# A conv and mixture-of-experts kernel: the first stage written in another order on four engines

## The reference

```
x = x + conv(ln_c(x))        # ln_c: mean and variance over the 192 channels
t = tokens(x)
t = t + ffn(ln_t(t))         # ln_t: the same over a token's 192 numbers
```

```
h   = xg @ W1[e]                     # 192 -> 1024
act = h[..., :512] * silu(h[..., 512:])
ye  = act @ W2[e]                    # 512 -> 192, weighted, added to the token
```

## Time and profile before

| | |
|---|---|
| median of three runs | 230.23 us (229.35 to 232.94) |
| the profiled execution | 229.77 us |
| its span, first to last instruction | 228.0 us |
| PE busy | 205.2 us (90%) |
| DVE busy | 160.2 us (70%) |
| ACT busy | 128.3 us (56%) |
| POOL busy | 118.7 us (52%) |
| mean granted clock of PE | 0.952 |

### The profile page before, as it was taken

How to read it: one execution, slowest core, us unless ns; L and a number is a source line. 1 busy time by engine, 2 the same in 40 slices (tenths; PEclk the granted TensorE clock), 3 DMA queues, 4 the chain that set the end, 5 groups by cost and what they waited for, 6 DMA issues and landing times.

```text
span 228.0 us, 4487 instructions
## 1 busy us (share of the span) xinstructions
PE 205.2 (90%) x1351; PEld 188.3 (83%) x1351; DVE 160.2 (70%) x509; ACT 128.3 (56%) x320; POOL 118.7 (52%) x130
## 2 busy tenths in 40 slices
PE   7998799869858999999999999999999999999930
PEld 2786699653327999999999999999999999999920
DVE  2674989998704599598598678679778868956520
ACT  2454765374202476587578578577568658745510
POOL 5102212100077154885877787687687683185184
PEclk9999999976795899999999999999999999999995
DMA  6648375879724392494395386288278253034043
GB/s 206 183 123 236 69 204 164 188 195 294 169 73 105 69 289 66 68 286 98 43 262 132 56 252 135 52 175 212 55 139 236 69 52 31 0 36 49 0 46 42
DMA packets 28015, 29.40 MB, mean 129 GB/s; under 512 B 6915, under 2 KB 24544, under 8 KB 28000
## 3 DMA queue, kind: packets, MB, share of 16 engines
q1 hardware_dynamic: 18656, 17.28, 26.6%
q0 software_dynamic: 7680, 9.05, 23.7%
q10 hardware_dynamic: 1664, 2.88, 4.8%
HBM read 19.86 MB, written 9.35 MB: 128 GB/s over the span
## 4 chain that ended last, share of the span: by engine, by line
PE 71%; DVE 11%; DMA 7%; POOL 3%; ACT 3%; issue 2%; SPq 1%; POOLq 0%; DVEq 0%; ACTq 0%
PE low L1173 6%; PE bank L1173 5%; PE first L1157 4%; PE first L1154 4%; PE first L1150 4%; PE first L1158 4%; PE first L1151 4%; PE low L1157 4%; PE low L1158 4%; PE low L1154 4%; PE low L1151 4%; PE low L1150 4%; PE both L1173 3%; PE low L1175 2%; PE bank L1175 2%
## 5 line engine op out<-in xcount | busy, mean ns | idle before, releaser
L500 POOL DMA_INDIRECT out<-y,goal x40 | 65.9, 1648 | 36.6 <-DVE y L933 27.4
L480 POOL DMA_INDIRECT rows<-rows_dram,source x40 | 42.5, 1062 | 36.2 <-DMA rows_dram<-row 18.9
L902 DVE TENSOR_TENSOR al<-act,ah 128x308 fp32r<-128x308 f32 x64 | 30.1, 471 | 1.0
L635 ACT CAST ah<-act 128x308 fp32r<-128x308 f32 x64 | 28.3, 443 | 1.8 <-DVE act L910 1.8
L910 DVE TENSOR_TENSOR act<-low,sil 128x308 f32<-128x308 f32 x32 | 15.3, 479 | 12.8 <-ACT sil L642 12.8
L642 ACT ACTIVATE sil<-first 128x308 f32<-128x308 f32 x32 | 13.7, 428 | 16.7 <-PE first L1158 15.6
L642 ACT ACTIVATE sil<-low 128x308 f32<-128x308 f32 x32 | 13.7, 428 | 14.2 <-PE low L1158 13.3
L910 DVE TENSOR_TENSOR act<-first,sil 128x308 f32<-128x308 f32 x32 | 15.3, 479 | 8.0 <-ACT sil L642 7.2
L1150 PE MATMUL first<-xh_a,hi_a 128*128 128x308 f32 x64 | 20.1, 314 | 0.7 <-ACT xh_a L625 0.7
L1157 PE MATMUL first<-x_b,hi_b 128*128 128x308 f32 x64 | 20.1, 314 | 0.0
L1154 PE MATMUL first<-xl_a,hi_a 128*128 128x308 f32 x64 | 19.9, 312 | 0.1
(11 more groups left out here) (172 smaller groups left out, 562.3 us busy)
## 6 DMA issues: line engine op xcount, KB each, us to landing
raw_b<-w SPq DMA_DIRECT2D x12, 256.0 KB, 4.1
raw_a<-w SPq DMA_DIRECT2D x6, 512.0 KB, 5.3
raw<-w SPq DMA_DIRECT2D x6, 384.0 KB, 6.1
gram_dram<-gram SPq DMA_DIRECT2D x8, 230.0 KB, 3.2
xt<-x_tokens SPq DMA_DIRECT2D x4, 384.0 KB, 4.4
out<-xt SPq DMA_DIRECT2D x4, 384.0 KB, 5.1
rows_dram<-row SPq DMA_DIRECT2D x3, 386.0 KB, 4.3
raw_b<-w ACTq DMA_DIRECT2D x4, 256.0 KB, 4.2
```

The costliest lines, as they stand in the source:

```text
L480: G.indirect_dma_start(out=rows[b][:, t, :], out_offset=None, in_=rows_dram, in_offset=bass.IndirectOffsetOnAxis(ap=source[:, n:n + 1], ax ...
L500: nc.gpsimd.indirect_dma_start(out=out, out_offset=bass.IndirectOffsetOnAxis(ap=goal[0:m, n:n + 1], axis=0), in_=y[0:m, t, :], in_offset=N ...
L635: nc.scalar.copy(ah[:, j, lo:hi], act[n % 3][:, 0:hi - lo]).then_inc(a_hi, 1)
L902: V.tensor_tensor(al[:, j, lo:hi], act[n % 3][:, 0:hi - lo], ah[:, j, lo:hi].bitcast(F32), ALU.subtract).then_inc(a_lo, 1)
```

## The change

Only stage 1 changes; every computation stays, but for the seven fillers.

- ACT: both halves of `take_gram(1)` and `deviation(3)` come before `take_corr(0)`, and the load of W1 of expert 0 behind it. The loads of expert 1 and `take_corr(3)` come before `deviation_b(2)` and `normed(2)`.
- PE: the 7 fillers after `grams(1)` go. `turn_corr(1)` stands between the halves of `grams(2)`.
- DVE: in the last group, `residual` and `stats_b` come ahead of the choice. `choose` is split in `best_scores` and the rest, `row_scales` in `row_shifts` and `row_gaps`.
- SP: `store_rows(2)` comes before `store_x1(1)`.

```diff
@@ SP
             store_x1(0)
+            store_rows(2)
             store_x1(1)
-            store_rows(2)
@@ ACT
             deviation(2)
+            take_gram(1)
+            deviation(3)
+            take_corr(0)
             load_w1(s, 0, 0)
-            take_gram(1, (0,))
-            take_corr(0)
-            deviation(3)
-            take_gram(1, (1,))
             features(2)
...
                 split_hi(0, 0, n)
-            deviation_b(2)
-            take_corr(3)
-            normed(2)
             load_w1(s, 1, 1)
             load_w2(s, 1, 1)
+            take_corr(3)
+            deviation_b(2)
+            normed(2)
@@ DVE
+            def best_scores(g):
                 for t in range(TILES):
                     last = V.max(top[:, t, :], score[:, t, :])
                 then(last)
+            def choose(g):
                 for t in range(TILES):
                     last = V.max_index(top_e[:, t, :], top[:, t, :], score[:, t, :])
...
                 combine(g)
-                choose(g)
-                residual(g)
-                stats_b(g)
                 if g + 1 < GROUPS:
+                    best_scores(g)
+                    choose(g)
+                    residual(g)
+                    stats_b(g)
                     find_slots(g)
-                    row_scales(g)
+                    row_shifts(g)
+                    row_gaps(g)
                 else:
-                    row_scales(g)
+                    residual(g)
+                    stats_b(g)
+                    best_scores(g)
+                    row_shifts(g)
+                    choose(g)
+                    row_gaps(g)
                     find_slots(g)
                 spots(g)
@@ PE
-            def grams(g):
+            def grams(g, halves=(0, 1)):
...
-                for t in range(TILES):
+                for t in [2 * h + i for h in halves for i in range(2)]:
...
             grams(1)
-            keep_busy(BUSY_FIRST, bank[0])
             turn_corr(0)
             conv_rest(0)
             turn_f(2)
             places(0)
-            grams(2)
+            grams(2, (0,))
             turn_corr(1)
+            grams(2, (1,))
```

More of the change, by code:

```diff
@@ L770, in stats_b @@
                 last.then_inc(var_b, 1)
-            def choose(g):
+            def best_scores(g):
                 for t in range(TILES):
@@ L806, in find_slots, with row_shifts @@
                 then(V.tensor_scalar(lane[:, :], slot[:, :], P - 1, None, ALU.bitwise_and))
-            def row_scales(g):
+            def row_shifts(g):
                 v.wait_ge(sqrt_b, g + 1)
@@ L813, in row_scales, with row_gaps @@
                                        in1=rstd_b[:, tiles(g)], op0=ALU.mult, op1=ALU.mult).then_inc(shift_ready, 1)
+            def row_gaps(g):
                 then(V.tensor_tensor(unit[:, :], norm[:, tiles(g)], rstd_b[:, tiles(g)], ALU.mult))
@@ L957, in _ @@
             T = nc.tensor
-            BUSY_START, BUSY_FIRST, BUSY_LAST, BUSY_TABLE, BUSY_END = 20, 7, 6, 14, 24
+            BUSY_START, BUSY_LAST, BUSY_TABLE, BUSY_END = 20, 6, 14, 24
             def keep_busy(n, idle):
```

## The result

The changed kernel takes **237.03 us** (median of 5, 234.59 to 237.31) against 230.23 (229.16 to 232.94): the ratio is 1.030 with a 95% interval of 1.025 to 1.035. I had forecast 231.2 and a range up to 233.6.

A forecast was written before the change was run, and what follows sets the result against it. It took the start of POOL's first gather to decide, released by the last row stores, with DVE's order from `conv_rest(1)` behind them. Sum: 229.77 - 0.4 + 1.9 - 0.1 = 231.2 us, range 228.2 to 233.6.

The forecast's parts named there:

- The rest: ACT's early loads of expert 1, `take_corr(3)` ahead of `deviation_b(2)`, SP's `store_rows(2)` first, fillers behind the table: summed as nothing.
- Part 1 and 2: Stage 1 up to `conv_rest(1)`: group 1's gram copied sooner, -0.4 us; PE's clock falling without the 7 fillers, +1.9 us.
- Part 1: Gram of group 1: second half copied 2.75 us sooner, so `conv_rest(1)` ends 0.4 us sooner, at 31.6.
- Part 3: Last group: row stores land at 60.6, but slow fillers delay row numbers to 61.65, which release the gather: -0.1 us.
- `near` of group 1 was late: Rival: W1 transfers delay `near` to 27.0, `conv_rest(1)` ends 0.5 us later at 32.6; 230.2 with clock held, chance 0.1.
- The slower case: Rival: PE's clock falls and stays low until group 2's convolution, PE becomes the bound: +5, 234.3 us, chance 0.12.

The follow-up runs named there:

- the last part alone: Kernel before with only the last group's `residual` and `stats_b` ahead of its choice, and `store_rows(2)` ahead of `store_x1(1)`: 232.97 us, ratio 1.011.

## Why the prediction was wrong

**The step that failed** is in "The rest": ACT's early loads of expert 1 were costed at nothing, "and a few tenths if `near(3)` is slowed, also under DVE's queue". The cover I named, DVE's queue, was only some 2.5 us deep: from `near(3)` at 42.9, the correlations (0.9), transposes (0.65), copy (0.6) and convolution (1.7) lead to 46.8, and DVE comes to group 3's scores at 49.3. It was used up by a transfer that I took to be slowed by tenths: `near(3)` was there at 50.7, 7.8 us later. Some 1.4 of these stood already when the gram went out, 3.8 came in its second store and 2.5 in the load of `near`. Then PE, idle for 5.28 us, made the transposes and the convolution at half clock, 2.1 us more than the 3.9 above. 7.8 - 2.5 + 2.1 is 7.4, and group 3's scores came 7.46 late. That last term, too, stands nowhere in my sum. I had the very row for the first, 4.9 against 2.6 us for a gram beside W1, and applied it to group 1 only. The loss is shown by undoing the loads (3.8 and 4.0 us back in the time), by doing them alone (from group 2's scores to group 3's 13.49 us in place of 8.60) and by issuing them on SP just behind `near(3)` (8.60 again). That the rows of group 0 add to it is shown by the landing of the gram's stores, 5.5 and 5.1 us with them ahead, 2.4 and 2.7 without. And behind `take_corr(3)`, `deviation_b(2)` was named as harmless; the run with the old order shows that it was.

**Part 1 and 2** were forecast together at +1.5, and `conv_rest(1)` ended 1.43 us late, at 33.50, with the clock at 0.50 for 6.8 us from 22.2 on. That the sum fits is luck, for both terms missed and the errors cancel. The run with the loads put back has the same front at full clock and ends `conv_rest(1)` at 32.32: so Part 1 is worth +0.25 and not -0.4, and the low stretch +1.2 and not +1.9. The cause I gave, the lost fillers, is not borne out as a cost: with them back the low stretch was half as long, and nothing came back. The gap of 1.65 us that the issues of W1 on ACT open before the features of group 2 is new too, but it is argued and not shown as the cause, since that same run has it and kept its clock.

Nor does the clock fall in the changed kernel alone. Of the six traces with its front and no fillers, five have a low stretch, of 6.8 us each, and one has none. Of the seven with the old front, four have none, the kernel before among them, and three have one of 3.4 us: the last part alone (0.50 between 27.3 and 30.7), the loads on SP (25.8 to 29.3) and the loads moved alone (26.5 to 29.9), whose rows read:

```profile
26.00:27.00 1.00, 0.63 (x2) 0.63 (x3) 0.96 (x4) 1.00 (x3) 0.00 (x0) 0.74 0.46 102
...
29.00:30.00 1.00, 1.00 (x6) 1.00 (x5) 0.68 (x5) 0.65 (x2) 0.44 (x2) 0.56 0.00 0
```

One profile is not enough to say whether a stretch keeps its clock, and two traces of different kernels can differ here by 2 us for no reason of their code.

**Part 3** had the mechanism in the changed kernel: the row numbers release the gather, 14 fillers run slowly behind `places(3)` (62.07 to 67.5), and PE has no idle time before the table. Its -0.1 measured -1.0 there, but the old order measured the same -1.0 beside early loads. With late loads the stores decide and land at 63.04 and not at 60.6, and the time is unchanged; the row numbers, ready at 61.64, came near the forecast of 61.65 (that trace comes to group 3's scores 0.4 us late). One more piece was mis-sized: I let the gather start 0.90 us after the later of its two releasers. After the stores it does; after the row numbers, ready at 68.87, it took 0.29.

**The rivals.** `near` of group 1 was late nearly as the rival said (26.4 for 27.0). In the changed kernel it held nothing, PE being slow itself. At full clock it did: in the run with the loads put back PE waited 0.68 us for the correlations, and `conv_rest(1)` ended at 32.32 (32.6 in the rival's text):

```profile
27.65 0.65 PE L1025 MATMUL bank<-cst,fc 128*93 128x128 f32 x4 [0.68 <-POOL fc L454]
```

The slower case was 234.3 by a clock that stays low, and the time passed even that: the right sign by the wrong mechanism.

## What to carry to other kernels

When an edit moves a transfer, list every transfer in flight at the new place, on all queues, and ask what waits for each; a price seen once in the trace (a store that took 4.9 us beside weights and 2.6 without) belongs to all of them. The 1.4 MB issued on the same queue behind the small round trip on which the chain rests cost nothing in the kernel before; issued by ACT two microseconds sooner, they cost some 4 us. A late transfer can cost twice, once by itself and once by the clock of the engine that idles for it. The largest wait of a profile need not be its cause: exchange the two instructions before you believe it. And before you lay a difference between two runs to an edit, find the place in the two traces where it arises; if it lies ahead of the edit, it is not the edit's.

## What the runs showed of the hardware

- Small transfers take up to three times as long beside bulk loads. 103 KB of `near` of group 3 took 3.9 to 6.6 us beside 1.4 MB of weights on ACT's queue, 2.0 to 2.9 with no weights about, and 2.0 to 3.7 with the weights behind it on SP's own. The Trainium skill, "DMA: Bandwidth & Descriptors", Queues, rings and completion order, has the engines go round the queues packet by packet. By this the load of `near` too should be slowed, and these traces now show the case that I had said was missing: 4.5 and 4.1 us for `near` of group 1 beside W1 in the changed kernel.
- The time of the 230 KB of gram of group 3 follows how far ahead the rows of group 0 (514 KB) went out. With no weights about, the first store took 5.5 to 5.8 us where their issue ended 0.2 to 0.4 us before it, 4.5 and 4.6 at 1.4 to 1.7 us, 3.2 to 3.9 at 2.0 to 2.5 us, and 2.4 without them. With the rows right ahead of it and weights behind it, it took 7.9 (7.1 and 7.3 in two of the experiments).
- POOL's first two gathers took 1.70 and 1.28 us where they began right behind the row numbers, while DVE was making the low parts of the weights (69.13 on), and 1.19 and 0.96 where DVE had done with them. With the loads of expert 1 on SP in the kernel before, the first gather began while DVE still made low parts and took 1.66, the second 0.96. That is not the whole rule: with the last part alone the first gather began at 65.85, 0.7 us before DVE had done, and took 1.18. No run was made to test it; in the changed kernel it is nearly all of the +0.90 of the account.
